# Degree products of the first layer's tail taken one part later, behind the dense product

## The reference

```python
agg = segment_sum(x[src], dst)              # sum of the source rows of each node's edges
deg = segment_sum(ones, dst)                # number of edges of each node
h = (agg / max(deg, 1)) @ Wl + bl + x @ Wr
```

## Time and profile before

| what | value |
|---|---|
| runs | median 4706.61 us of 3 (4705.94 to 4712.58) |
| profiled execution, time | 4704.45 us |
| profiled execution, span from first to last instruction | 4702.6 us |
| instructions | 62658 |
| mean granted TensorE clock | 0.840 |
| busy | PE 3601.8 us (77%), DVE 1966.6 (42%), ACT 666.1 (14%), POOL 3178.1 (68%) |
| DMA | 896.10 MB, mean 191 GB/s |
| chain that ended last | PE 42%, issue 17%, POOL 13%, DVE 13%, DMA 10% |
| L952, PE's degree matmuls | 416, idle before them 149.8 us, all for DVE's L1295 |
| L964, PE's dense matmuls of the first layer | 444 records into `big`'s buffers, mean 702 ns |

### The profile page before, as it was taken

One profiled execution on the slowest core, in us unless ns is written; L12 is line 12 of the kernel. 1 busy time (PEld: TensorE's weight loads), 2 busy tenths in 40 slices (PEclk: granted clock), 3 DMA queues, 4 the chain that ended last, 5 costly groups with the idle time before them and its releaser, 6 DMA issues.

```text
span 4702.6 us, 62658 instructions
## 1 busy us (share of the span) xinstructions
PE 3601.8 (77%) x16020; PEld 2336.4 (50%) x16020; DVE 1966.6 (42%) x5344; ACT 666.1 (14%) x1712; POOL 3178.1 (68%) x3027
## 2 busy tenths in 40 slices
PE   3346666666658887598999999999896888888876
PEld 1234333333434444586666666666584444444446
DVE  4546777778755555652222222222171222222212
ACT  3001234444420000141000000000012000000002
POOL 2778888778875555315777777777644777777774
PEclk6567888888778888698999899999898888888887
DMA  6212444555679876237676676676659887888886
GB/s 171 60 51 69 145 171 180 193 197 224 229 241 231 207 207 174 97 130 233 202 207 204 200 211 200 203 208 201 207 156 281 217 221 208 217 218 223 209 221 197
DMA packets 928868, 896.10 MB, mean 191 GB/s; under 512 B 62823, under 2 KB 832505, under 8 KB 921754
## 3 DMA queue, kind: packets, MB, share of 16 engines
q1 hardware_dynamic: 819210, 643.90, 46.2%
q0 software_dynamic: 106432, 250.27, 18.4%
q10 hardware_dynamic: 3152, 1.06, 0.1%
HBM read 683.01 MB, written 211.98 MB: 190 GB/s over the span
## 4 chain that ended last, share of the span: by engine, by line
PE 42%; issue 17%; POOL 13%; DVE 13%; DMA 10%; DVEq 3%; SPq 1%; ACT 1%; POOLq 0%; ACTq 0%
PE ps L1082 15%; POOL ring L699 13%; PE ps L930 12%; DMA ring<-table,idx_now 7%; DVE area L1398 5%; PE ps L964 4%; DVE big L1267 2%; PE ps L944 2%; PE ps L1124 2%; PE ps L1109 2%; DVEq L1270 2%; DVE area L1295 1%; DVE wrong L1292 1%; PE ps L952 1%; DMA table<-area 1%
## 5 line engine op out<-in xcount | busy, mean ns | idle before, releaser
L699 POOL DMA_INDIRECT ring<-table,idx_now x2836 | 3024.1, 1066 | 1174.7 <-issue 912.3
L1267 DVE TENSOR_TENSOR big<-big,ps 128x32 f32 (+1 forms) x2836 | 567.4, 200 | 2350.8 <-PE ps L930 1958.8
L1082 PE MATMUL ps<-area 128*128 128x512 f32 (+1 forms) x2744 | 1386.6, 652 | 23.9 <-DMA area<-table 23.0
L930 PEld LDWEIGHTS ps<-onehot,ring 128*128 128x128 f32 x7632 | 1035.3, 211 | 733.6 <-issue 708.4
L930 PE MATMUL ps<-onehot,ring 128*128 128x32 f32 x7632 | 1023.6, 289 | 484.3 <-DMA ring<-table,idx_now 243.9
L1082 PEld LDWEIGHTS ps<-area 128*128 128x128 f32 x2744 | 556.2, 215 | 565.4 <-issue 542.1
L944 PE MATMUL ps<-area 128*128 128x392 f16 x2208 | 519.4, 395 | 218.0 <-DVE area L1398 216.5
L1398 DVE TENSOR_TENSOR area<-iota_code,area 128x3136 f16<-128x3136 f16 (+4 forms) x568 | 649.3, 1205 | 46.4 <-PE ps L944 43.0
L803 ACT ACTIVATE idx_now<-idx_all 128x5 int32 (+3 forms) x608 | 125.0, 207 | 3179.9 <-PE ps L930 3168.5
L944 PEld LDWEIGHTS ps<-area 128*128 128x128 f16 x2208 | 237.0, 115 | 468.3 <-DVE area L1398 261.2
L816 ACT ACTIVATE big<-ps 128x392 f32<-128x392 f32 x736 | 351.6, 498 | 407.8 <-PE ps L944 405.8
(11 more groups left out here) (138 smaller groups left out, 1503.8 us busy)
## 6 DMA issues: line engine op xcount, KB each, us to landing
edge_count<-big SPq DMA_DIRECT2D x46, 3136.0 KB
area<-edge_count SPq DMA_DIRECT2D x98, 1472.0 KB
area<-edge_count SPq DMA_DIRECT2D x98, 960.0 KB
big<-edge_count SPq DMA_DIRECT2D x37, 1536.0 KB, 7.8
ring<-table,idx_now POOLq DMA_INDIRECT x2836
area<-table SPq DMA_DIRECT2D x98, 256.0 KB
ring<-input SPq DMA_DIRECT2D x98, 256.0 KB, 2.7
input<-ring SPq DMA_DIRECT2D x48, 512.0 KB, 3.9
```

The source lines that it names most:

```text
L699: pool.indirect_dma_start(out=ring[:, g * n + j, 0:width], out_offset=None, in_=table[layer][:, :], in_offset=bass.IndirectOffsetOnAxis(ap ...
L930: last = nc.tensor.matmul(to[:, m * W:(m + 1) * W], ring[:, k, m * P:(m + 1) * P], onehot[:, k, :], start=True, stop=True)
L1082: last = nc.tensor.matmul(dense_ps(layer, f, k)[:, 0:(end - h) * HB].rearrange("p (h c) -> p h c", c=HB), unit_rows[b][layer][:, s, f * P: ...
L1267: V.tensor_tensor(sums, sums, step, ALU.add).then_inc(s_acc[layer], 1)
```

## The change

Three edits. In `tail` on PE the degree product is taken in parts 1 and 3 in place of 0 and 2, and behind the dense product, so it stands one part and two dense products later than before against the same work on DVE; for this each of its matmuls increments a new semaphore, and DVE waits for the last of them behind the last body. The read of the degrees from PSUM (L1509) moves ahead of the branch, with a second copy inside the branch. On POOL, two semaphores that nobody waits for become an existing one, which nobody waits for either.

```diff
@@ semaphores
-        s_part = [sem(f"s_part{layer}") for layer in range(3)]
+        s_degree_sum = sem("s_degree_sum")
-        s_late_begin = sem("s_late_begin")
@@ gather, gather_late (POOL)
-                        pool.sem_inc(s_part[layer], 1)
+                        pool.sem_inc(s_begin, 1)
...
-                    pool.sem_inc(s_late_begin, 1)
+                    pool.sem_inc(s_begin, 1)
@@ sum_degrees (PE)
                 for c in range(KCH):
                     nc.tensor.matmul(degree_ps, hots[:, c, P:P + BLOCKS], hots[:, c, 0:P],
                                      start=isinstance(w, int) and w == 0 and c == 0,
-                                     stop=isinstance(w, int) and w == W - 1 and c == KCH - 1, skip_group_check=True)
+                                     stop=isinstance(w, int) and w == W - 1 and c == KCH - 1, skip_group_check=True
+                                     ).then_inc(s_degree_sum, 1)
@@ tail (PE)
             def tail(g, w, unit, turn):
-                if w is not None:
-                    sum_degrees(w, g // 2)
                 if unit is not None:
                     first_dense(g, unit, turn)
+                if g % 2 == 1:
+
+                    sum_degrees(turn * 2 + (g // 2 - 2), g // 2)
@@ behind the bodies (DVE)
             dve.wait_ge(s_acc[0], BODIES[0] * PER_BODY[0])
 
+
+            dve.wait_ge(s_degree_sum, W * KCH)
+            link(V.tensor_scalar(degrees[0:BLOCKS, :], degree_ps, 1.0, None, ALU.max))
             dve.sem_inc(s_degree, 1)
             with if_irregular(dve):
...
+                link(V.tensor_scalar(degrees[0:BLOCKS, :], degree_ps, 1.0, None, ALU.max), s_sort)
...
-
-            link(V.tensor_scalar(degrees[0:BLOCKS, :], degree_ps, 1.0, None, ALU.max))
             V.reciprocal(degrees[0:BLOCKS, :], degrees[0:BLOCKS, :]).then_inc(s_inv, 1)
```

## The result

The changed kernel takes 4568.9 us (median of 4 runs, 4568.75 to 4569.74) against 4706.27 of the kernel before (4 runs): a ratio of 0.9703, 95% interval 0.9688 to 0.9717, 137 us less. 4575 was forecast.

What follows compares the result with a forecast made beforehand. PE and DVE waiting for each other in a ring were taken as the bound, with DMA next; 123.7 us (first stretch) + 8.2 (second) = 131.9 off 4704.45 gives 4572.5, 4575 for the median, range 4550 to 4625.

Steps and rivals of the forecast that it cites:

- The wait and its cover: First stretch, PE's degree product: one-hots ready after 9.5 us, asked for after 18.8, so the wait goes.
- The price of a part: First stretch, with a dense product in every part: 7.2 us a part against 9.74, 123.7 us less.
- the allowance for jitter: First stretch: a little on top of the 7.05 us DMA floor, giving 7.2 a part; buffers mostly take jitter up.
- The other floors: First stretch, per part: PE 6.83 us, POOL 6.76, SP 6.87, within 0.3 us of DMA's 7.05.
- The second stretch: Tail windows without dense product: DVE runs through without waiting for PE, 96.9 to 88.7 us, 8.2 less.
- The sum: Whole kernel: 123.7 + 8.2 = 131.9 us off 4704.45 gives 4572.5, so 4575 for the median.
- the term for the end: End of the tail, last degree product and the moved read of the degrees: zero, at worst 1 us.
- A: First stretch: PE waits for unit loads and its clock falls, 8.1 us a part, median 4618; chance 0.14.
- B: First stretch: loads carry more than 288 GB/s, PE bounds at 6.83 us a part, 4552 to 4557; chance 0.06.
- C: First stretch: gathered rows come late behind units, 10.7 us a part, median 4743, slower; chance 0.03.
- D: PE meets the one-hots unready again and waits as before, time stays at 4707; chance 0.02.
- The signs named ahead: First stretch about 350 us, DMA share near 1.1, near 280 GB/s, clock over 0.95, POOL over 70%, DVE's wait some 60.

Runs made afterwards that it cites:

- the two experiments on the order: Changed kernel with the degree product only moved behind the dense product, same part: 4578.4 us; only taken a part later, ahead of the dense product: 4570.5 us.
- no degrees: Changed kernel with all work on the degrees (one-hots and products) left out, all degrees taken as 1: 4552.3 us.
- the half loads: Changed kernel with half of the counts of each unit left unloaded: 4565.5 us.

## Why the prediction was right

**The wait and its cover.** DVE's one-hots were to be 9 us early. In the window shown they are done at 1610.90, 9.5 us after DVE starts on the odd sums at 1601.36, and PE takes them at 1620.71, 9.8 us later. There is no wait left, and the two experiments on the order, which by their expectations ask for them 11.6 and 12.8 us after the odd sums instead of 18.8, show no such wait in the first stretch either. The step was right with room to spare.

**The price of a part.** The forecast took the DMA floor of 7.05 us "and a little", 7.2. Measured are 7.01. The rate of 288 GB/s, read from the 60 us in which the loads had run back to back, was the right row; the allowance for jitter was not needed: 48 x 0.19 = 9 us of the first stretch (351.0 forecast, 342.0 measured), the one term of the sum that was clearly mis-sized. That the four buffers take the jitter up is likely and was not tested. The other floors: PE's 6.83 measured 6.69 with the loads relieved. POOL's 6.76, read from ten gathers of one window, was too low: in the changed kernel 241 gathers take 256.4 us and their usual gaps 77.7, 6.93 a part, only 0.08 under the loads. It was not the bound, since the stretch stays at 341.5 us with POOL relieved (no degrees), but it leaves little to win behind the loads. SP's 6.87 was the loads' own. The Trainium skill's limit of some 358 GB/s (DMA: Bandwidth & Descriptors, Specifications) would have put the bound on PE and POOL. The plateau lies at 290 GB/s: in this mix of 512-byte rows the loads bind first, well under that limit.

**The second stretch.** 8.2 us less forecast, 7.4 measured. DVE's waits for PE are gone there but for one, and PE still waits for DVE (36.6 us in 7 waits), both as said. PE also waits twice for gathered rows:

```profile
PE ps L929 <- DMA ring<-table,idx_now: 4.3, 2, 3.5
...
DVE big L1268 <- PE ps L929: 2.9, 1, 2.9
```

POOL, said to have room there (81 us of gathers), is in truth busy without a break but its usual gaps of 0.3 to 0.5 us until 1819.7 us, 10 us before ACT copies the sums; DVE and POOL end nearly together.

**The sum.** Forecast 131.9, measured in the profiled executions 132.7 + 7.4 = 140.1 for the tail, and 135.6 for the span, since this execution's tail started 9.9 us later, its first unit came 0.4 sooner and its rest was 5.0 shorter. The later start is hardly the change's: the first issue lies at 1379 to 1388 us in the three executions with the old order and at 1383 to 1393 in the ten with the new one. For the rest it stays open. From ACT's copy to DVE's inverse of the degrees it is 3.37 us before and 3.33 after, so the term for the end, zero, was right; but the rest as a whole is 2740.2 to 2742.4 with the old order and 2737.4 to 2740.7 with the new one. So that 4575 came within 6 us of 4568.9 is in part luck: the gain of the tail was put 8 us too low, and the tail happened to start late.

**The rivals.** A (waits for loads let the clock fall): the waits are there, 20 of 0.34 us, and the clock stays at 0.99. Waits of that size did not make it fall here; behind the one of 1.66 us in the earlier trace rows, from 2320 to 2328 us, it was at 0.59 and 0.55. B (PE bounds): fell, by the half loads. C (gathered rows late): not one such wait in the first stretch at a share of 1.15. D (the one-hots are unready again) fell: no row of that wait is left in the first stretch. The signs named ahead held: first stretch 342.0 us for about 350, share 1.15 for 1.1, 285 GB/s for 280, clock 0.99 for over 0.95, POOL busy 75% for over 70%; DVE's wait for PE is 64.3 - 17.8 = 46.5 us without the first, where 60 was expected.

**Left open.** Why the stretches ahead of the tail move by up to 13 us between executions, and the rest by 5, was not tried, nor what the second stretch and the tail would take with POOL's gathers alone made cheaper.

## What to carry to other kernels

Where two engines wait for each other in a ring, look for the consumer that can take its input one step later: no work has to shrink, only the order. Then price the new step by every floor that stands behind the wait, DMA rate included, because a ring hides them all; here loads, POOL and PE lay at 7.01, 6.93 and 6.69 us a part, and the gain of relieving the first of them went mostly back a stage later. A long issue time on a DMA queue can be the loads' own bound and no second one (6.12 us here, 0.58 with half the loads). A wait of PE can cost twice, by itself and by the clock behind it: 78 and 55 us here.

## What the runs showed that I had not expected

- Work with no use made a kernel faster: 14 matmuls a window in PE's wait, 60 us less.
- The DMA queues hold 287 to 293 GB/s in 39 of 40 slices over 342 us with gathers and unit loads mixed, and PE waits for no gather meanwhile.
- Leaving half of the unit loads away saved 15.5 us in one stretch and cost 11.9 in the next, because POOL, which has next to no idle time from the start of the tail to its end, had issued 8 gathers fewer by then (233 against 241).
